# Two-layer graph attention block, one core: the score matmuls of the two layers are placed elsewhere among the projections, and layer 2's gather stands two matmuls later

## Chip, cores and metric

One Trainium2 chip, one of its NeuronCores. The metric is the device time of one execution in microseconds (us), the median over runs. The kernel holds 128 graphs of 128 nodes with 384 features each, all in float32, with the matmul operands split into two float32r parts.

## What is computed

For each graph with features h (128 x 384) and adjacency matrix A, two layers of

```
u     = h h^T / sqrt(384)
attn  = softmax(u) * A, each row divided by its sum
ctx   = (attn above the diagonal) (h Wl^T + bl) + diag(attn) (h Ws^T + bs)
        + (attn below the diagonal) (h Wr^T + br)
h'    = relu(layernorm(ctx) * g + beta)
```

and at the end `layernorm(x + h')`. The second layer reads the first one's output, so the two layers of one graph are dependent and different graphs are not.

## The kernel before, in words

Each engine has a program of its own, written out by hand and tied to the others by semaphores. All of them go through the same rounds i = 0 ... 132. A round works on layer 1 of graph i and on layer 2 of graph i-3 or so; the rounds 0 to 3 fill the pipeline, 127 on drain it, rounds 8 to 123 stand in a hardware loop unrolled four times. In this text k = 0 is layer 1 and k = 1 is layer 2, as in the code.

**TensorE in a round** (`iteration` of the tensor block) issues, before the change:

1. `project_sides(0, i)`: 18 projection matmuls of layer 1 (128x384 moving), nine for the upper and nine for the lower side. Each product of two float32 matrices is three matmuls on float32r parts (high x high, low x high, high x low), times three chunks of the 384 features.
2. `project_self(0, i)`: nine more for the self term. Among them `pair_slice` puts the score steps: matmuls 2, 3, 4 are each followed by one step of layer 1's scores of graph i+2, matmuls 5, 6, 7 each by one step of layer 2's scores of graph i-2. A score step (`score_step`, line 458) is one matmul with 256 moving columns over one of the three chunks.
3. `project_sides(1, i-3)`, steps 0 to 6; then `gather(1, i-4)`, six matmuls that apply layer 2's attention; then steps 7 to 17 of the same sides.
4. `project_self(1, i-3)`, nine matmuls; then `gather(0, i)`, six matmuls.

That makes 54 projections (line 464), 12 gather matmuls (line 584) and 6 score steps (line 458). Waits are put before the matmul that needs them: `gather(1, i-4)` waits for POOL's low part of the cut attention (`s_side_lo[1]`, line 1289) and for the low part of the projections; the score steps wait for the low part of the features that they read (`s_lo[0]` written by POOL at line 1319 for layer 1, `s_lo[1]` written by VectorE at line 745 for layer 2) and for `s_kept`, which says that ScalarE has copied the PSUM bank of the last scores away.

**VectorE in a round**: `normalise_layer1(i-1)` (lines 689 to 708), `low_rows(i-2)` (line 745), the bias of layer 1's sides (line 758, which waits for the last matmul of `project_sides(0, i)`), the scaled scores of both layers (line 769), a transposition, the masks (line 793) with their transpositions, the diagonals, and then the second half: the self bias, layer 2's rows (lines 689 to 716) after `gather(1)`, layer 2's bias (758), `output_rows` (724, 730), the self bias of layer 2 (762).

**ScalarE in a round**: the rectified rows (line 1074), their high part (1085), `normalise_rows` (1057), the two exponentials (1030), `high_sides(1, i-4)` (1044), `copy_cross(i)` (1016), `high_projections(0, i)` (1053), `high_sides(0, i)` (1044), `keep_high(i)` (1024, 1025; it raises `s_kept`), the load of transposed rows, `high_input` (1124; the high part of a new graph's features), small ones, `finish` (1057), `high_projections(1, i-3)` (1053).

**POOL in a round**: `low_projections(1, i-4)` (line 299), the layer norm's root and bias, the sum of crossed scores (1345), the cuts of both attention matrices (1283), `low_sides(1, i-4)` and `low_sides(0, i)` (1289), `low_projections(0, i)` (299), two more roots (1293), and at the end `low_input` (1319; the low part of a new graph's features).

**SyncE** issues the transfers in order; the features of graph i+4 (`xt_raw<-xT`) are asked for at the start of round i, once `s_lo[0]` of graph i+2 is there.

The high part of graph i+3's features is made by ScalarE in round i, its low part by POOL at the end of round i; four slots (`hT_layer1`) hold them.

Of the kernel before, what the change touches and what calls it, by code (L numbers as in the profile page):

```python
# [52 lines left out]
def graph_block(nc: bass.Bass, xT: bass.AP, x: bass.AP, adj: bass.AP, WT: bass.AP, bias: bass.AP,  # L53
                gain_cols: bass.AP, shift_cols: bass.AP, gain_row: bass.AP, shift_row: bass.AP, out: bass.AP):
    G, N, D = x.shape
    C = D // P
# [6 lines left out]
    with ExitStack() as ctx:  # L63
# [129 lines left out]
        def per_layer(name):  # L193
            return [sem(f"{name}1"), sem(f"{name}2")]
# [3 lines left out]
        s_lo = per_layer("s_lo")  # L198
        s_parts = per_layer("s_parts")
# [6 lines left out]
        s_kept = sem("s_kept")  # L206
# [37 lines left out]
        def live(i, b):  # L244

            return not isinstance(i, int) or 0 <= b < G

        def done(eng, s, b):

            if not isinstance(b, int) or b >= 0:  # L250
                eng.wait_ge(s, b + 1)
# [43 lines left out]
        def low_projections(op, eng, k, b):  # L295

            u = unit(k, b)
            done(eng, s_proj_hi[k], b)
            op.tensor_tensor(proj_split[u][:, LO], proj[u][:, UP:LOW + 1, :],  # L299
                             proj_split[u][:, HI].bitcast(F32), ALU.subtract).then_inc(s_proj_lo[k], 1)  # L300

        def filling(i):

            return isinstance(i, int) and i < 4
# [149 lines left out]
        def _(pe):  # L454
            def score_step(k, b, slot, n):

                h = hT_of(k, b)
                return nc.tensor.matmul(parts[k], h[:, slot, HI, n, :],  # L458
                                        h[:, slot, HI:LO + 1, n, :], start=(n == 0), stop=(n == C - 1))

            def project_step(k, b, slot, which, n):

                c, (mv, st) = n // 3, TERMS[n % 3]
                return nc.tensor.matmul(p_proj[:, which, 0:D], hT_of(k, b)[:, slot, st, c, :],  # L464
                                        w[:, k, which, mv, c, :], start=(n == 0), stop=(n == 8))
# [16 lines left out]
                    nc.tensor.matmul(parts[k][:, HI, :], cross[k][:], ident_r[:], start=False,  # L482
                                     stop=True, skip_group_check=True).then_inc(s_score[k], 1)

            def pair_slice(b0, slot0, b1, slot1, n):

                if n == 2:
                    if isinstance(b1, int) and b1 == 2:  # L490
                        done(pe, s_negmax[0], 5)
                        done(pe, s_negmax[1], 1)
                    else:
                        done(pe, s_kept, b1 - 3)
                    if b0 is not None:
                        done(pe, s_lo[0], b0)
                if b0 is not None and 2 <= n < 2 + C:
                    step = score_step(0, b0, slot0, n - 2)
                    if n == 1 + C:
                        step.then_inc(s_parts[0], 1)  # L500
                if n == 2 + C:
                    done(pe, s_lo[1], b1)
                if 2 + C <= n < 2 + 2 * C:
                    step = score_step(1, b1, slot1, n - 2 - C)
                    if n == 1 + 2 * C:
                        step.then_inc(s_parts[1], 1)

            def project_sides(k, b, slot, before, b_last, steps, scored=None, first=0, last_part=14):

                if 0 in steps:
                    done(pe, s_biased[before], b_last)
                for n in steps:
                    if isinstance(b, int) and b == 0 and n % 3 == 0:

                        pe.wait_ge(s_w_lo[k][UP + n // 9], n % 9 // 3 + 1)
                    last = project_step(k, b, slot, UP + n // 9, n % 9)
                    if scored is not None:  # L520
                        score_slice(*scored, n, first, last_part)
                if 17 in steps:
                    last.then_inc(s_proj[k], 1)

            def project_self(k, b, slot, before, b_last, scored=None, first=0, last_part=8, pair=None):
                done(pe, s_self_biased[before], b_last)
                for n in range(9):
                    if isinstance(b, int) and b == 0 and n % 3 == 0:
                        pe.wait_ge(s_w_lo[k][SELF], n // 3 + 1)
                    last = project_step(k, b, slot, SELF, n)  # L530
                    if pair is not None:
                        pair_slice(*pair, n)
                    if scored is not None and n < 8:
                        score_slice(*scored, n, first, last_part)
                last.then_inc(s_self[k], 1)
                if scored is not None:
                    score_slice(*scored, 8, first, last_part)
# [122 lines left out]
            def iteration(i, r):  # L660
                p, q = r % 2, 1 - r % 2
                if filling(i):
                    fill(i, p)
                elif closing(i):
                    close(i, p)
                else:
                    b0 = i + 2 if live(i, i + 2) else None
                    project_sides(0, i, r, 1, i - 4, range(18))
                    project_self(0, i, r, 1, i - 4, pair=(b0, (r + 2) % 4, i - 2, p))
                    project_sides(1, i - 3, q, 0, i, range(7))  # L670
                    gather(1, i - 4)
                    project_sides(1, i - 3, q, 0, i, range(7, 18))
                    project_self(1, i - 3, q, 0, i)
                    gather(0, i, True)

# [328 lines left out]
        def _(act):  # L1004
# [115 lines left out]
            def high_input(b, slot):  # L1120
                moved(act, s_xt, b, slot % 2)

                done(act, s_self[0], b - 4)
                nc.scalar.activation(hT[0][:, slot, HI], xt_raw[:, slot % 2], ACT.Copy).then_inc(s_hi[0], 1)  # L1124
# [123 lines left out]
            def iteration(i, r):  # L1248
                p, q = r % 2, 1 - r % 2
                if filling(i):  # L1250
                    fill(i, p, q)
                    return
                if closing(i):
                    close(i, p, q)
                    return
                relu_rows(i, i - 2, p)
                high_rows(i - 2, p)
                normalise_rows(i, i - 1)
                exponentials(1, i - 3, q)
                if live(i, i + 1):  # L1260
                    exponentials(0, i + 1, q)
                high_sides(1, i - 4)
                copy_cross(i)
                high_projections(0, i)
                high_sides(0, i)
                keep_high(i)
                load_rows(i - 1, q)
                if live(i, i + 3):
                    high_input(i + 3, (r + 3) % 4)
                if live(i, i + 1):  # L1270
                    squared_denominators(0, i + 1, q)
                squared_denominators(1, i - 3, q)
                if live(i, i - 5):
                    output_squares(i - 5, q)
                    finish(i, q)
                high_projections(1, i - 3)
# [4 lines left out]
        def _(pool):  # L1281
# [4 lines left out]
            def low_sides(k, b):  # L1286
                u = unit(k, b)
                done(pool, s_side_hi[k], b)
                nc.gpsimd.tensor_tensor(AT_split[u][:, LO], AT[u][:], AT_split[u][:, HI].bitcast(F32),  # L1289
                                        ALU.subtract).then_inc(s_side_lo[k], 1)  # L1290
# [26 lines left out]
            def low_input(b, slot):  # L1317
                done(pool, s_hi[0], b)
                nc.gpsimd.tensor_tensor(hT[0][:, slot, LO], xt_raw[:, slot % 2], hT[0][:, slot, HI].bitcast(F32),  # L1319
                                        ALU.subtract).then_inc(s_lo[0], 1)  # L1320
# [87 lines left out]
            def iteration(i, r):  # L1408
                p, q = r % 2, 1 - r % 2
                if filling(i):  # L1410
                    fill(i, p, q)
                    return
                if closing(i):
                    close(i, p, q)
                    return
                low_projections(nc.gpsimd, pool, 1, i - 4)
                deviation_layer1(i - 1)
                attn_arrived(i - 1, q)
                if not isinstance(i, int) or i > 4:
                    add_cross(0, 2)  # L1420
                cut_sides(1, i - 4)
                cut_sides(0, i)
                low_sides(1, i - 4)
                low_sides(0, i)
                low_projections(nc.gpsimd, pool, 0, i)
                deviation_layer2(i - 4)
                if live(i, i - 5):
                    deviation_output(i - 5, q)
                if live(i, i + 3):
                    low_input(i + 3, (r + 3) % 4)  # L1430

            run(pool, iteration)

# [31 lines left out]
```

## Time and profile before

| | |
|---|---|
| median of 3 runs | 1624.32 us (1623.67 to 1625.14) |
| the profiled execution's own time | 1624.36 us |
| its span, first to last instruction | 1622.6 us |
| granted TensorE clock | 0.998 |
| busy: TensorE, VectorE, ScalarE, POOL | 99%, 86%, 67%, 80% |
| projections, gathers, score steps | 6912, 1536, 768 matmuls |

How to read it: PE is TensorE's matmuls, PEld its weight loads, DVE VectorE, ACT ScalarE. In a timeline row the columns are start and duration in us, engine, line, operation, what is written and read, the shape, and how many instructions of one kind in a row were merged (x21); a bracket tells how long the engine was idle before and what ended that. A matmul's recorded duration (0.34 us for 384 columns) is longer than the distance to the next one's start, since they are pipelined; so the pace of n merged matmuls is (duration - 0.34) / (n - 1).

### The profile page before, as it was taken

How to read it: one execution, taken by the hardware profiler on the slowest of the kernel's cores; microseconds unless marked ns; L12 is line 12 of the kernel's file. 1: busy time of each engine (PE TensorE's matmuls, PEld its weight loads, DVE VectorE, ACT ScalarE, POOL GpSimd, SP SyncE). 2: the span in 40 equal slices, each digit the busy share in tenths (PEclk: the TensorE clock that was granted, in tenths of full speed). 3: DMA queues.
4: the chain of work that ended last, by engine and by line, in shares of the span. 5: the costliest groups of instructions: out<-in, count | busy, mean ns of one | idle time of the engine just before them, and what ended most of it. 6: DMA issues, size and time to landing. Idle time of an engine off the chain costs nothing.

```text
span 1622.6 us, 35792 instructions
## 1 busy us (share of the span) xinstructions
PE 1604.5 (99%) x9267; PEld 1579.7 (97%) x9267; DVE 1397.6 (86%) x4490; ACT 1079.5 (67%) x2958; POOL 1294.3 (80%) x1665
## 2 busy tenths in 40 slices
PE   9999999999999999999999999999999999999996
PEld 8999999999999999999999999999999999999995
DVE  7888888888888888888888888888888888888887
ACT  6666666666666666666666666666666666666665
POOL 6788888888878888888888888888888888888874
PEclk9999999999999999999999999999999999999999
DMA  5555555555555555555555555555555555555541
GB/s 184 124 138 130 132 128 139 127 132 128 139 126 133 129 137 126 134 134 131 131 130 133 131 134 128 134 132 134 128 137 130 132 128 139 127 133 129 133 107 49
DMA packets 589175, 211.28 MB, mean 130 GB/s; under 512 B 473952, under 2 KB 572256, under 8 KB 589152
## 3 DMA queue, kind: packets, MB, share of 16 engines
q1 hardware_dynamic: 490752, 198.91, 47.5%
q10 hardware_dynamic: 98400, 12.11, 4.8%
q8 instruction: 9, 0.15, 0.0%
q14 instruction: 14, 0.11, 0.0%
HBM read 128.98 MB, written 81.92 MB: 130 GB/s over the span
## 4 chain that ended last, share of the span: by engine, by line
PE 96%; POOL 1%; DVE 1%; ACT 1%; issue 1%; DMA 0%; ACTq 0%; DVEq 0%; SPq 0%; POOLq 0%
PE p_proj L464 73%; PE p_gather L584 17%; PE p_score L458 5%; POOL proj_split L299 0%; DMA w_raw<-WT 0%; POOL w L1340 0%; POOL rstd L1293 0%; ACT proj_split L1053 0%; DMA rows_mem<-rows_blocks 0%; POOL attnT_split L1289 0%; DVE proj L758 0%; ACT spread L1112 0%; DVE p_gather L716 0%; ACT p_score L1030 0%; DVE p_gather L724 0%
## 5 line engine op out<-in xcount | busy, mean ns | idle before, releaser
L464 PE MATMUL p_proj<-w,hT_layer 128*128 128x384 f32 x6912 | 1352.5, 339 | 0.0
L464 PEld LDWEIGHTS p_proj<-w,hT_layer 128*128 128x128 f32 x6912 | 1221.7, 188 | 0.2
L299 POOL TENSOR_TENSOR proj_split<-proj,proj_split 128x768 fp32r<-128x768 f32 x253 | 467.2, 1846 | 88.1 <-ACT proj_split L1053 88.1
L584 PE MATMUL p_gather<-proj_split,attnT_split 128*128 128x384 f32 x1536 | 324.0, 345 | 1.8 <-issue 1.5
L758 DVE TENSOR_TENSOR proj<-p_proj,bias_all 128x768 f32<-128x768 f32 x256 | 243.8, 952 | 79.1 <-PE p_proj L464 79.0
L1289 POOL TENSOR_TENSOR attnT_split<-attnT,attnT_split 128x256 fp32r<-128x256 f32 x256 | 189.8, 741 | 152.3 <-ACT attnT_split L1044 152.2
L584 PEld LDWEIGHTS p_gather<-proj_split,attnT_split 128*128 128x128 f32 x1536 | 264.7, 188 | 23.3 <-POOL attnT_split L1289 21.2
L1293 POOL TENSOR_TENSOR rstd<-veps,neg_half 128x1 f32<-128x1 f32 x384 | 209.5, 549 | 56.3 <-DVE veps L702 40.7
L1053 ACT ACTIVATE proj_split<-proj 128x768 fp32r<-128x768 f32 x256 | 213.0, 832 | 5.2 <-DVE proj L758 4.2
L458 PE MATMUL p_score<-hT_layer 128*128 128x256 f32 x768 | 215.2, 281 | 1.1 <-DVE hT_layer L745 0.8
L1057 ACT ACTIVATE normed<-gathered,nbias,rstd 128x384 f32<-128x384 f32 x128 | 90.7, 709 | 140.3 <-POOL nbias L1297 140.3
L1057 ACT ACTIVATE o<-y,nbias,rstd 128x384 f32<-128x384 f32 x128 | 90.8, 709 | 133.0 <-POOL nbias L1297 133.0
L1283 POOL TENSOR_TENSOR attnT<-whole,sides 128x256 f32<-128x256 f32 x249 | 178.8, 739 | 0.3 <-DMA whole<-swap_mem 0.3
L1124 ACT ACTIVATE hT_layer<-xt_raw 128x384 fp32r<-128x384 f32 x128 | 67.2, 525 | 144.7 <-issue 143.7
L1074 ACT ACTIVATE p_rows<-rowsT,shift,gain 128x128 f32<-128x128 f32 x369 | 149.4, 444 | 0.0
L1030 ACT ACTIVATE p_score<-scores,rows 128x128 f32<-128x128 f32 x256 | 92.8, 363 | 83.8 <-DVE rows L769 83.8
L458 PEld LDWEIGHTS p_score<-hT_layer 128*128 128x128 f32 x768 | 144.9, 189 | 1.9 <-DVE hT_layer L745 1.1
L762 DVE TENSOR_TENSOR proj<-p_proj,bias_all 128x384 f32<-128x384 f32 x256 | 141.5, 553 | 1.8 <-PE p_proj L464 1.7
L1319 POOL TENSOR_TENSOR hT_layer<-xt_raw,hT_layer 128x384 fp32r<-128x384 f32 x128 | 131.3, 1026 | 2.5 <-ACT hT_layer L1124 2.5
L793 DVE CUSTOM_DVE_ANT_0 attn<-p_score,adj_layer 128x128 f32<-128x128 f32 x256 | 70.9, 277 | 44.6 <-ACT p_score L1030 42.4
L1044 ACT ACTIVATE attnT_split<-attnT 128x256 fp32r<-128x256 f32 x256 | 103.3, 403 | 0.5 <-DVE attnT L822 0.5
L689 DVE SCALAR_TENSOR_TENSOR p_gather<-proj,rows,p_gather 128x384 f32<-128x384 f32 x128 | 79.6, 622 | 19.9 <-PE p_gather L584 12.5
(69 smaller groups left out, 1677.7 us busy)
## 6 DMA issues: line engine op xcount, KB each, us to landing
swap_mem<-blocks SPq DMA_DIRECT2D x124, 256.0 KB, 2.2
whole<-swap_mem SPq DMA_DIRECT2D x496, 64.0 KB, 2.5
xt_raw<-xT SPq DMA_DIRECT2D x128, 192.0 KB, 2.8
xn<-x SPq DMA_DIRECT2D x128, 192.0 KB, 2.7
out<-o SPq DMA_DIRECT2D x128, 192.0 KB, 2.0
rows_mem<-rows_blocks SPq DMA_DIRECT2D x123, 192.0 KB, 1.9
adj_layer<-adj SPq DMA_DIRECT2D x256, 64.0 KB, 2.1
rowsT<-rows_mem SPq DMA_DIRECT2D x246, 48.0 KB, 2.6
```

The costliest lines, as they stand in the source:

```text
L299: op.tensor_tensor(proj_split[u][:, LO], proj[u][:, UP:LOW + 1, :], proj_split[u][:, HI].bitcast(F32), ALU.subtract).then_inc(s_proj_lo[k], 1)
L458: return nc.tensor.matmul(parts[k], h[:, slot, HI, n, :], h[:, slot, HI:LO + 1, n, :], start=(n == 0), stop=(n == C - 1))
L464: return nc.tensor.matmul(p_proj[:, which, 0:D], hT_of(k, b)[:, slot, st, c, :], w[:, k, which, mv, c, :], start=(n == 0), stop=(n == 8))
L584: last = nc.tensor.matmul(home(k, b)[:, 0:D], AT_split[u][:, st, side, :], proj_split[u][:, mv, side, :], start=(side == UP and n == 0), s ...
L758: nc.vector.tensor_tensor(proj[u][:, UP:LOW + 1, :], p_proj[:, UP:LOW + 1, 0:D], bias_all[:, k, UP:LOW + 1, :], ALU.add).then_inc(s_biased ...
L762: nc.vector.tensor_tensor(proj[u][:, SELF, :], p_proj[:, SELF, 0:D], bias_all[:, k, SELF, :], ALU.add).then_inc(s_self_biased[k], 1)
L1053: nc.scalar.activation(proj_split[u][:, HI], proj[u][:, UP:LOW + 1, :], ACT.Copy).then_inc(s_proj_hi[k], 1)
L1057: nc.scalar.activation(rows_out, rows_in, ACT.Identity, bias=nbias[:, which:which + 1], scale=rstd[:, which:which + 1]).then_inc(s_rows, 1)
L1074: last = nc.scalar.activation(relu_T[:, c, :], rows_in[:, c, :], ACT.Relu, bias=shift1[:, c:c + 1], scale=gain1[:, c:c + 1])
L1283: nc.gpsimd.tensor_tensor(AT[k][:], whole[:, k].unsqueeze(1).broadcast_to([P, 2, N]), sides[:], ALU.mult).then_inc(s_side[k], 1)
L1289: nc.gpsimd.tensor_tensor(AT_split[u][:, LO], AT[u][:], AT_split[u][:, HI].bitcast(F32), ALU.subtract).then_inc(s_side_lo[k], 1)
L1293: return nc.gpsimd.tensor_tensor(rstd[:, which:which + 1], veps[:, which:which + 1], neg_half[:], ALU.pow)
```

## The change

The score steps are taken out of `pair_slice` and spread:

- Layer 1's scores of a graph take three steps in three places. The first (chunk 0) for graph i+3 is issued in round i, behind matmul 9 of `project_sides(1, i-3)`, which is the first after `gather(1, i-4)`. The other two (chunks 1 and 2), for graph i+2, follow matmuls 1 and 3 of `project_sides(0, i)`. In rounds 4 and 5 all three stand in `project_sides(0, i)`, behind matmuls 1, 3 and 5.
- Layer 2's three steps (graph i-2) follow matmuls 0, 1 and 2 of `project_self(0, i)`.
- `gather(1, i-4)` follows steps 0 to 8 of `project_sides(1, i-3)`, not 0 to 6.
- The features are prepared a graph earlier: `high_input` and `low_input` work in round i on graph i+4, not i+3. In round 4 both do graph 7 too, POOL's before `low_projections(0, 4)`.

```diff
-            def pair_slice(b0, slot0, b1, slot1, n):
-                if n == 2:
...
+            def score_early(b0, slot0, chunk):
+                if chunk == 0:
+                    done(pe, s_lo[0], b0)
+                    if isinstance(b0, int) and b0 == 6:
                         done(pe, s_negmax[0], 5)
                         done(pe, s_negmax[1], 1)
                     else:
+                        done(pe, s_kept, b0 - 7)
+                step = score_step(0, b0, slot0, chunk)
+                if chunk == C - 1:
+                    step.then_inc(s_parts[0], 1)
+
+            def score_late(b1, slot1, n):
+                if n == 0:
+                    done(pe, s_lo[1], b1)
+                    if not isinstance(b1, int) or b1 > 2:
                         done(pe, s_kept, b1 - 3)
+                if n < C:
+                    step = score_step(1, b1, slot1, n)
+                    if n == C - 1:
                         step.then_inc(s_parts[1], 1)
...
                     last = project_step(k, b, slot, UP + n // 9, n % 9)
+                    if early is not None and (n, early[2]) == (9, 0):
+                        score_early(early[0], early[1], 0)
+                    if early is not None and n in (1, 3, 5) and early[2] > 0 and n // 2 + early[2] <= C:
+                        score_early(early[0], early[1], n // 2 + early[2] - 1)
...
-                    b0 = i + 2 if live(i, i + 2) else None
-                    project_sides(0, i, r, 1, i - 4, range(18))
-                    project_self(0, i, r, 1, i - 4, pair=(b0, (r + 2) % 4, i - 2, p))
-                    project_sides(1, i - 3, q, 0, i, range(7))
+                    alone = isinstance(i, int) and i < 6
+                    rest = (i + 2, (r + 2) % 4, 1 if alone else 2) if live(i, i + 2) else None
+                    first = (i + 3, (r + 3) % 4, 0) if live(i, i + 3) and not (isinstance(i, int) and i < 5) else None
+                    project_sides(0, i, r, 1, i - 4, range(18), early=rest)
+                    project_self(0, i, r, 1, i - 4, late=(i - 2, p))
+                    project_sides(1, i - 3, q, 0, i, range(9))
                     gather(1, i - 4)
-                    project_sides(1, i - 3, q, 0, i, range(7, 18))
+                    project_sides(1, i - 3, q, 0, i, range(9, 18), early=first)
                     project_self(1, i - 3, q, 0, i)
                     gather(0, i, True)
...
                 load_rows(i - 1, q)
-                if live(i, i + 3):
-                    high_input(i + 3, (r + 3) % 4)
+                if isinstance(i, int) and i == 4:
+                    high_input(7, 3)
+                if live(i, i + 4):
+                    high_input(i + 4, r)
...
                 low_sides(0, i)
+                if isinstance(i, int) and i == 4:
+                    low_input(7, 3)
                 low_projections(nc.gpsimd, pool, 0, i)
...
-                if live(i, i + 3):
-                    low_input(i + 3, (r + 3) % 4)
+                if live(i, i + 4):
+                    low_input(i + 4, r)
```

## Rows read from the trace of the kernel before

**Rows 1.** The page: busy time by engine, and TensorE's clock in 40 slices.
```profile
PE 1604.5 (99%) x9267; PEld 1579.7 (97%) x9267; DVE 1397.6 (86%) x4490; ACT 1079.5 (67%) x2958; POOL 1294.3 (80%) x1665
...
PEclk9999999999999999999999999999999999999999
```

**Rows 2.** Who waited for whom: us in total, times, longest.
```profile
DVE proj L758 <- PE p_proj L464: 79.0, 128, 1.0
...
PEld p_gather L584 <- POOL attnT_split L1289: 21.2, 122, 0.5
```

**Rows 3.** Timeline of TensorE in one round, which begins at 802.67.
```profile
802.67 3.87 PE L464 MATMUL p_proj<-w,hT_layer 128*128 128x384 f32 x21
...
806.38 0.28 PE L458 MATMUL p_score<-hT_layer 128*128 128x256 f32 x1
...
807.96 1.55 PE L464 MATMUL p_proj<-w,hT_layer 128*128 128x384 f32 x8
...
809.36 1.33 PE L584 MATMUL p_gather<-proj_split,attnT_split 128*128 128x384 f32 x6
...
810.54 3.70 PE L464 MATMUL p_proj<-w,hT_layer 128*128 128x384 f32 x20
...
814.07 1.21 PE L584 MATMUL p_gather<-proj_split,attnT_split 128*128 128x384 f32 x6
...
815.12 1.22 PE L464 MATMUL p_proj<-w,hT_layer 128*128 128x384 f32 x6
```

**Rows 4.** The same round, what stands between its sides and layer 2's gather.
```profile
806.05 0.96 DVE L758 TENSOR_TENSOR proj<-p_proj,bias_all 128x768 f32<-128x768 f32 x1 [0.63 <-PE p_proj L464]
...
806.99 0.28 DVE L769 CUSTOM_DVE_ANT_0 scores<-p_gather,cross_sum 128x128 f32<-128x128 f32 x1
...
807.31 0.37 ACT L1030 ACTIVATE p_score<-scores,rows 128x128 f32<-128x128 f32 x1 [0.68 <-DVE rows L769]
...
808.10 0.40 ACT L1044 ACTIVATE attnT_split<-attnT 128x256 fp32r<-128x256 f32 x1
...
808.57 0.73 POOL L1289 TENSOR_TENSOR attnT_split<-attnT,attnT_split 128x256 fp32r<-128x256 f32 x1 [0.61 <-ACT attnT_split L1044]
...
809.36 1.01 PEld L584 LDWEIGHTS p_gather<-proj_split,attnT_split 128*128 128x128 f32 x6 [0.17 <-POOL attnT_split L1289]
```

**Rows 5.** The same round: layer 2's new features, and the end of the kept scores.
```profile
804.86 0.56 DVE L745 TENSOR_TENSOR hT_layer<-p_rows,hT_layer 128x384 fp32r<-128x384 f32 x1
...
809.90 0.22 ACT L1025 ACTIVATE p_gather<-p_score 128x128 f32<-128x128 f32 x1
```

**Rows 6.** Timeline of TensorE elsewhere: projections in a row, start-up and drain.
```profile
14.73 2.76 PE L464 MATMUL p_proj<-w,hT_layer 128*128 128x384 f32 x15
```
```profile
1574.17 5.11 PE L464 MATMUL p_proj<-w,hT_layer 128*128 128x384 f32 x28
...
1580.05 0.28 PE L458 MATMUL p_score<-hT_layer 128*128 128x256 f32 x1
1580.17 0.86 PE L464 MATMUL p_proj<-w,hT_layer 128*128 128x384 f32 x4
```
```profile
19.73 0.87 PE L464 MATMUL p_proj<-w,hT_layer 128*128 128x384 f32 x4
```

**Rows 7.** Round 4: ScalarE's and POOL's end of the round, and layer 1's gather.
```profile
51.17 1.85 POOL L299 TENSOR_TENSOR proj_split<-proj,proj_split 128x768 fp32r<-128x768 f32 x1
...
53.80 1.01 POOL L1319 TENSOR_TENSOR hT_layer<-xt_raw,hT_layer 128x384 fp32r<-128x384 f32 x1
```
```profile
52.79 0.53 ACT L1124 ACTIVATE hT_layer<-xt_raw 128x384 fp32r<-128x384 f32 x1 [2.06 <-issue]
```
```profile
54.69 1.21 PE L584 MATMUL p_gather<-proj_split,attnT_split 128*128 128x384 f32 x6
```

**Rows 8.** Round 6: the latest of layer 2's new features, and the round's start.
```profile
70.96 0.56 DVE L745 TENSOR_TENSOR hT_layer<-p_rows,hT_layer 128x384 fp32r<-128x384 f32 x1 [0.61 <-ACT hT_layer L1085]
```
```profile
68.17 3.87 PE L464 MATMUL p_proj<-w,hT_layer 128*128 128x384 f32 x21
```

More of the change, by code:

```diff
@@ L483, in score_slice @@
                                      stop=True, skip_group_check=True).then_inc(s_score[k], 1)
-            def pair_slice(b0, slot0, b1, slot1, n):
-                if n == 2:
-                    if isinstance(b1, int) and b1 == 2:
+            def score_early(b0, slot0, chunk):
+                if chunk == 0:
+                    done(pe, s_lo[0], b0)
+                    if isinstance(b0, int) and b0 == 6:
                         done(pe, s_negmax[0], 5)
@@ L493, in pair_slice, with project_sides @@
                     else:
-                        done(pe, s_kept, b1 - 3)
[L495 to L505, printed above, removed]
+                        done(pe, s_kept, b0 - 7)
[6 more added lines that the diff above has]
+                    if not isinstance(b1, int) or b1 > 2:
+                        done(pe, s_kept, b1 - 3)
+                if n < C:
+                    step = score_step(1, b1, slot1, n)
+                    if n == C - 1:
                         step.then_inc(s_parts[1], 1)
-            def project_sides(k, b, slot, before, b_last, steps, scored=None, first=0, last_part=14):
+            def project_sides(k, b, slot, before, b_last, steps, scored=None, first=0, last_part=14,
+                              early=None):
                 if 0 in steps:
@@ L523, in project_sides, with project_self @@
                     last.then_inc(s_proj[k], 1)
-            def project_self(k, b, slot, before, b_last, scored=None, first=0, last_part=8, pair=None):
+            def project_self(k, b, slot, before, b_last, scored=None, first=0, last_part=8, late=None):
                 done(pe, s_self_biased[before], b_last)
@@ L530, in project_self @@
                     last = project_step(k, b, slot, SELF, n)
-                    if pair is not None:
-                        pair_slice(*pair, n)
+                    if late is not None:
+                        score_late(*late, n)
                     if scored is not None and n < 8:
```

## Prediction, made before the changed kernel was run

> **What bounds the kernel now.** The page comes first: TensorE is busy 99% of the span, at its full clock in every slice (the higher of its two levels, 2.4 GHz), the next engine 86% [rows 1]. So only two things can give time back: a place where TensorE waits, and the pace at which its matmuls follow each other. The list of waits shows the one wait that comes back in every round: the weight load of layer 2's gather stands until POOL has written the low part of the cut attention, 21.2 us in 122 times, 0.17 us each [rows 2]. TensorE's timeline shows what that costs: layer 2's gather takes 1.33 us where layer 1's, which waits for nothing, takes 1.21 [rows 3]. So 0.12 us of a round are lost (the remaining 0.05 of the late load hide behind the running matmul), 122 x 0.12 = 14.6 us in all. A round lasts 815.12 - 802.67 = 12.45 us [rows 3].
>
> Then the pace. Projections in a row follow each other at (3.87 - 0.34) / 20 = 0.1765 us at the round's start and at (3.70 - 0.34) / 19 = 0.1768 behind layer 2's gather, but at (1.55 - 0.34) / 7 = 0.1729 behind the last score step [rows 3]. I call these the slow and the fast pace; they differ by 0.0037 us. The fast one is no matter of layer or weights: in the start-up 15 projections of layer 1 run at (2.76 - 0.34) / 14 = 0.1729, and in the drain 28 in a row run at (5.11 - 0.34) / 27 = 0.1767 and, once three score steps have come between, at (0.86 - 0.34) / 3 = 0.173 [rows 6]. One row speaks against a simple rule: behind the scores that follow a gather in the start-up, four run at (0.87 - 0.34) / 3 = 0.177 [rows 6]. A score step costs this: from 806.38 to 807.96 are six of them and five projections, 1.58 us, less 5 x 0.1765, by six: 0.116 us [rows 3].
>
> **The change part by part.** No matmul is added or removed: 54 P, 12 gathers and 6 scores stay in a round. P is 0.1765 and S is 0.116.
>
> *The gather, two steps later, and the scores ahead of it.* What does the gather wait for? Rows 4, read upwards: POOL's operation waited for ScalarE, which waited for VectorE's scores, which follow its bias addition with no pause, and that one had been idle for 0.63 us until TensorE's last matmul of layer 1's sides. This wait is there 128 times [rows 2]. The last of those 18 matmuls starts at 802.67 + 17 x 0.1765 = 805.67 and ends 0.34 later, 806.01; the gather's load starts at 809.36. So the gather is ready 3.35 us after the end of the sides, whatever TensorE does between. Before, TensorE would have wanted that load at 33 P + 6 S = 6.52 us of the round and had it at 6.69: 0.17 late, as the row says. After, two scores stand inside the sides, so all that chain starts 2 S = 0.23 later and the load is ready at 6.92. TensorE wants it at 35 P + 5 S = 6.76: 0.16 late. Two projections put in front (0.35) are paid back by one score that leaves that stretch (0.12) and two that delay the chain (0.23). The stall stays: 0 us, with 0.01 x 122 = 1.2 us as the most that the rounding of these rows allows either way.
>
> *Everything behind shifts alike.* VectorE's work behind layer 2's gather, and what ScalarE and POOL do after it, moves 0.23 later in the round, and so does the end of layer 1's sides that it must be ready for: the 0.63 us of idle time [rows 4] stays. SyncE's queue asks for no other transfers, and at the same places; its wait on `s_lo[0]` only gets easier. Cost 0, covered by that 0.63.
>
> *New waits.* (a) Layer 2's first score follows projection 0 of the self term and waits for VectorE's low rows. They end at 804.86 + 0.56 - 802.67 = 2.75 in the round, 3.04 after the shift and a signal of 0.06; TensorE wants the weights at 18 P + 2 S = 3.41. There are 0.37 us to spare, where there was about 1 us. Cost 0; behind it in TensorE's queue stands all of the rest. (b) The early score behind the gather waits for ScalarE's kept scores, which end at 809.90 + 0.22 = 810.12, 0.76 after the gather's load starts [rows 4, 5]; TensorE wants the weights when the projection ahead of the score starts, 1.18 after it (810.54 in this round [rows 3]). Both hang on the same chain, so 1.18 - 0.76 - 0.06 = 0.36 us stay. Cost 0. (c) POOL's low input for it was made a round before. Cost 0. ScalarE's `high_input` now needs the self term of the same round, which ended at about 807.96 plus one and a half projections; it runs at 811.3. Cost 0.
>
> *The pace.* This is the term that I take to be worth something. In layer 1's sides two scores now stand behind matmuls 1 and 3, in the position of the drain's case (slow before, fast after [rows 6]), so matmuls 4 to 17 should run at the fast pace: 14 x 0.0037 = 0.05 us a round, in 121 rounds (5 to 125) 6.3 us; I take 6.1, one round less sure at each end. A faster pace between the sides and the gather gives nothing, for the gather waits for the chain. Behind the gather stands one score; if the 15 projections behind it ran fast too, that would be 15 x 0.0037 x 121 = 6.7 us more. That one is nearest the start-up row which stayed slow, so I count 0 and keep 6.7 for the range. Nothing excludes a loss: a score costs up to 0.120 in place of 0.116, 121 x 2 x 0.004 = 1 us.
>
> What the rows show here is a projection at 0.1729 or at 0.1767 by what ran before it. The Trainium skill (TensorE: Matmul & The Clock Gate, section Wait — 56ns, not 53.3ns?) says otherwise: back-to-back matmuls are N / 2.4 GHz plus a fixed 2.5 ns or so, 162.5 ns for 384 columns. By that rule no order of scores changes the pace, and the term would be 0. The trace agrees with neither the size nor the fixedness.
>
> *Round 4, once.* POOL makes graph 7's low input before `low_projections(0, 4)`. It can begin when ScalarE's copy ends, 52.79 + 0.53 = 53.32, takes 1.01 and ends at 54.33; the projections' low part takes 1.85, to 56.18, where it began at 51.17 before. Layer 1's gather, which wanted its weights at 54.69 - 0.17 = 54.52, gets them 1.7 us late [rows 7]. Cost 1.7 us; bounds 0 (if the rounds behind catch up) and 2.5 (if the roots queued behind on POOL, and VectorE's output rows that wait for them, are late in round 5 too).
>
> **Sum.** Against the profiled execution's own 1624.36 us (span 1622.6 and 1.8 around it; the median of the runs is 1624.32, so nothing is to be moved): -6.1 + 1.7 = -4.4, **1620.0 us**.
>
> **The rivals.**
> - *Both paces turn fast.* -6.1 - 6.7 + 1.7: 1613.3 us. For it: a fast stretch in the start-up lasts 15 matmuls. Against it: the row at 19.73 [rows 6]. Chance 0.22.
> - *The pace does not hang on the scores.* Then nothing is left but round 4 and the score's own price: 1624.4 + 1.7, 1626.1 us (to 1627). For it: slow behind scores in the start-up; the skill's rule would say the same. Against it: 122 rounds with 0.1729 behind the last score. Chance 0.27.
> - *The change does what its words suggest.* The gather's two steps hide its wait: 14.6 us off, 1624.4 - 14.6 + 1.7 = 1611.5 us. It needs a chain that does not start at the sides' end; 128 waits of VectorE for TensorE speak against it. Chance 0.05.
> - *Slower: the late scores wait for the low rows.* Place: the first score in `project_self(0, i)`. It decides once VectorE ends line 745 more than 0.37 us later in the round than now, which happened in round 6: 70.96 + 0.56 - 68.17 = 3.35 [rows 8]. If every round were like it: ready at 3.35 + 0.23 + 0.06 = 3.64, 0.23 late, 0.16 of it seen; 0.12 is given back at the gather, which has that much less to wait, and since the gather's chain hangs on the sides only 0.04 to 0.09 a round are left, 5 to 11 us: 1632 us beside the pace's rival. Chance 0.08.
>
> **How the numbers follow.** The forecast has 0.38. The range takes in it, the two pace rivals with round 4's bounds, and most of the hidden wait: 1612.5 to 1627.5, leaving out the slower case and the far ends. About 0.2% (3.2 us) is what a measurement of this kernel can tell from no change, so faster means below 1621.1. The forecast lies only 1.1 us under that, so a quarter of its chance counts as same: faster 0.28 + 0.22 + 0.05 = 0.55; same 0.10 + 0.23 = 0.33; slower 0.04 + 0.08 = 0.12.
>
> **What would show it.** In the changed profile: TensorE's row behind the second score in layer 1's sides, 15 projections (14 and the self term's first) at 0.173 and not 0.177; the weight load of layer 2's gather still idle before it for 0.16 to 0.19 us, 121 times, on POOL; VectorE's 0.6 us idle before line 758 as before; a round of 12.40 us; and once, at about 55 us, a wait of 1.7 us for POOL's line 299. Wrong I would be if that load's wait were gone, if scores waited on VectorE's line 745 or ScalarE's 1025, or if the pace in the sides stayed at 0.1765.

## The result, and the profile after

The changed kernel takes 1614.55 us (median of 6 runs, 1613.59 to 1615.10) against 1624.43 us of the kernel before on the same chips (1623.67 to 1625.42): ratio 0.9938, 95% interval 0.9925 to 0.9950. That is 9.9 us less, where the forecast was 4.4 less (1620.0 us) and the range 1612.5 to 1627.5.

The page of the changed kernel, against [rows 1]:

```profile
span 1613.0 us, 35972 instructions
...
PE 1594.6 (99%) x9267; PEld 1571.5 (97%) x9267; DVE 1396.4 (87%) x4490; ACT 1079.3 (67%) x2958; POOL 1294.1 (80%) x1665
```

The matmuls are the same 9267, and 9.9 us of TensorE's busy time are gone. "Busy" is the union of pipelined matmuls here, so this is a change of pace, which no list of waits shows. The waits, against [rows 2]:

```profile
DVE proj L767 <- PE p_proj L464: 71.6, 127, 1.1
...
PEld p_gather L591 <- POOL attnT_split L1300: 14.3, 92, 0.2
```

VectorE still waits for the end of layer 1's sides, 71.6 / 127 = 0.56 us a round (79.0 / 128 = 0.62 before). The weight load of layer 2's gather still waits for POOL. The longest single wait is 0.2 us; it is listed 92 times, but the gather is late in every round: its second matmul starts 0.269 us or more behind the first in all 119 rounds that are compared below, and 0.176 us (median) behind it where the stall is gone (experiment 3). One round on TensorE's timeline, against [rows 3], and then its weight load:

```profile
802.89 2.81 PE L464 MATMUL p_proj<-w,hT_layer 128*128 128x384 f32 x15
805.54 1.32 PE L591 MATMUL p_gather<-proj_split,attnT_split 128*128 128x384 f32 x6
...
806.99 3.17 PE L464 MATMUL p_proj<-w,hT_layer 128*128 128x384 f32 x17
810.00 1.21 PE L591 MATMUL p_gather<-proj_split,attnT_split 128*128 128x384 f32 x6
811.05 0.52 PE L464 MATMUL p_proj<-w,hT_layer 128*128 128x384 f32 x2
...
811.99 2.76 PE L464 MATMUL p_proj<-w,hT_layer 128*128 128x384 f32 x15
814.59 0.28 PE L458 MATMUL p_score<-hT_layer 128*128 128x256 f32 x1
```
```profile
805.54 0.99 PEld L591 LDWEIGHTS p_gather<-proj_split,attnT_split 128*128 128x128 f32 x6 [0.16 <-POOL attnT_split L1300]
```

Layer 1's sides with the first self matmul, 19 projections and two scores, take 814.59 - 811.05 = 3.54 us; at the slow pace they would take 19 x 0.1765 + 2 x 0.116 = 3.59. The fifteen behind the second score run at (2.76 - 0.34) / 14 = 0.1729. Behind the late scores, which have one projection between them, fifteen run at (2.81 - 0.34) / 14 = 0.1764: that stretch was fast before and is slow now. The gather takes 1.32 us, 0.11 more than layer 1's: its stall is there (before: 0.12), and the load is 0.16 us late, as forecast. Behind it 17 projections run at (3.17 - 0.34) / 16 = 0.177 in this round. In five of the six rounds from 607 to 674 us, though, that row is shorter; one of each kind:

```profile
609.30 3.12 PE L464 MATMUL p_proj<-w,hT_layer 128*128 128x384 f32 x17
...
621.65 3.17 PE L464 MATMUL p_proj<-w,hT_layer 128*128 128x384 f32 x17
```

3.12 is (3.12 - 0.34) / 16 = 0.1738 a projection: fast. The last twelve projections of that row run at 0.1733 in 84 of the 119 rounds and at 0.1767 in the other 35. Over all unrolled and looped rounds (119 after, 122 before) the mean start-to-start times add up as follows, in us:

| stretch of a round | before | after | plain slow pace would give after |
|---|---|---|---|
| layer 1's sides, with the scores in them | 3.181 | 3.371 | 3.181 + 0.232 = 3.413 |
| from there to the gather's second matmul | 3.800 | 3.802 | |
| the rest of the gather | 0.885 | 0.879 | |
| from the gather to layer 1's gather | 3.535 | 3.264 | 3.535 - 2 x 0.1765 + 0.116 = 3.298 |
| layer 1's gather | 1.046 | 1.044 | |
| sum | 12.446 | 12.360 | |

The second line is the chain: two projections more and three scores fewer stand in that stretch, and it lasts the same to 0.002 us. The experiments show why: the gather is bound by what began at the sides' end. The change's gain lies in the first and fourth lines, 0.042 and 0.034 us of pace, plus 0.006 in the gather; that is 0.082 of the 0.086 us, and the rest is no more than P and S are rounded by. 0.086 x 120 = 10.3 us, less one wait of 0.9 us in round 4, gives 9.4 of the 9.9 us. The wait:

```profile
50.68 1.21 PE L591 MATMUL p_gather<-proj_split,attnT_split 128*128 128x384 f32 x6
...
55.81 1.28 PE L591 MATMUL p_gather<-proj_split,attnT_split 128*128 128x384 f32 x6 [0.74 <-issue]
```

### The profile page after: what moved, and what is told of

Same layout as the page of the kernel before. It is cut to its first block, busy times and chain, and to the rows that moved or that the text cites. A ratio compares the mean times of both kernels' runs of the same rounds, so it can differ in the third digit from the quotient of the medians.

```text
span 1613.0 us, 35972 instructions
## 1 busy us (share of the span) xinstructions
PE 1594.6 (99%) x9267; PEld 1571.5 (97%) x9267; DVE 1396.4 (87%) x4490; ACT 1079.3 (67%) x2958; POOL 1294.1 (80%) x1665
## 4 chain that ended last, share of the span: by engine, by line
PE 97%; DVE 1%; POOL 1%; ACT 1%; issue 0%; DMA 0%; SPq 0%; DVEq 0%; POOLq 0%; ACTq 0%
PE p_proj L464 74%; PE p_gather L591 17%; PE p_score L458 5%; DMA w_raw<-WT 0%; POOL proj_split L299 0%; POOL w L1351 0%; DVE proj L767 0%; DVE p_gather L725 0%; DVE p_gather L733 0%; DVE stats L702 0%; DVE p_gather L698 0%; ACT proj_split L1062 0%; PE p_score L482 0%; DVE y L739 0%; POOL rstd L1304 0%
## 5 line engine op out<-in xcount | busy, mean ns | idle before, releaser
L464 PEld LDWEIGHTS p_proj<-w,hT_layer 128*128 128x128 f32 x6912 | 1193.7, 188 | 0.5 <-POOL w L1351 0.3
L767 DVE TENSOR_TENSOR proj<-p_proj,bias_all 128x768 f32<-128x768 f32 x256 | 243.9, 953 | 71.6 <-PE p_proj L464 71.6
```

Source lines behind the costliest of these rows:

```text
L767: nc.vector.tensor_tensor(proj[u][:, UP:LOW + 1, :], p_proj[:, UP:LOW + 1, 0:D], bias_all[:, k, UP:LOW + 1, :], ALU.add).then_inc(s_biased ...
```

## Experiments

Two theories stood against each other. **Chain and pace**: layer 2's gather is ready a fixed time after the end of layer 1's sides; the gain comes from which projections run at the fast pace. **Gather**: the gain comes from the gather's later place, as the change's words suggest.

**1. The gather back in its old place.** One edit to the changed kernel:

```diff
-                    project_sides(1, i - 3, q, 0, i, range(9))
+                    project_sides(1, i - 3, q, 0, i, range(7))
                     gather(1, i - 4)
-                    project_sides(1, i - 3, q, 0, i, range(9, 18), early=first)
+                    project_sides(1, i - 3, q, 0, i, range(7, 18), early=first)
```

> The changed kernel with layer 2's gather back behind 7 sides matmuls, all else as changed. Theory (the gather is ready a fixed 3.35 us after the end of layer 1's sides, and two scores stand in those sides): TensorE reaches the gather two projections (0.35 us) earlier and waits that much longer, 0.10 + 0.35 = 0.45 us a round, 121 x 0.35 = 42 us more than the changed kernel's 1614.6: 1657 us. Rival (the gain is the pace alone and the gather's place is of no account): 1615 us. Second rival (the gather's readiness moves with what TensorE does just before it, not with the sides' end): 1615 to 1625 us.

Measured: 1655.72 us (1655.48 to 1656.31), ratio to before 1.0189 (1.0174 to 1.0205). Its weight loads:

```profile
800.89 1.00 PEld L591 LDWEIGHTS p_gather<-proj_split,attnT_split 128*128 128x128 f32 x6 [0.50 <-POOL attnT_split L1300]
```

The load is 0.50 us late, where it was 0.16, and 41.2 us were lost where 42 were forecast. The gather does not get ready any sooner when TensorE comes sooner. By the mean round the stretch from the sides' end to the gather's second matmul is 3.805 us, against 3.802 in the changed kernel. So the two steps are no gain of their own: they pay for the two scores put ahead of the sides' end and the one that left the stretch.

**2. The gather's move alone**, in the kernel before:

```diff
-                    project_sides(1, i - 3, q, 0, i, range(7))
+                    project_sides(1, i - 3, q, 0, i, range(9))
                     gather(1, i - 4)
-                    project_sides(1, i - 3, q, 0, i, range(7, 18))
+                    project_sides(1, i - 3, q, 0, i, range(9, 18))
```

> The kernel before with only layer 2's gather moved behind 9 sides matmuls; the scores stay in the self term. Theory: nothing stands in layer 1's sides, so the gather is ready at the same time and TensorE reaches it 0.35 us later, after it is ready: the 0.12 us of stall go, the pace stays slow: 1624.4 - 122 x 0.12 = 1610 us, a round of 12.33 us. Rival (the gather's readiness slides with TensorE): the load's wait stays, 1624 us. Rival (VectorE becomes the bound, since layer 2's second half starts 0.23 us later in the round): 1615 to 1625 us with waits of TensorE for line 758 or 745.

Measured: 1607.59 us (1606.68 to 1608.15) against 1624.73 before, ratio 0.9895 (0.9880 to 0.9910). Its weight-load waits and a round:

```profile
PEld p_gather L584 <- POOL attnT_split L1289: 0.6, 3, 0.3
```

```profile
811.71 1.90 PE L464 MATMUL p_proj<-w,hT_layer 128*128 128x384 f32 x10
813.44 1.20 PE L584 MATMUL p_gather<-proj_split,attnT_split 128*128 128x384 f32 x6
```

122 waits have become 3 and the gather takes 1.20 us. Without scores ahead of the sides' end the move does hide the stall, and this one edit is worth 17.1 us, more than the whole change. That is 2.5 us more than the 14.6 forecast. The mean round is 12.303 us, 0.142 less than before (0.142 x 122 = 17.3 us). Of this the gather gives 0.120, as forecast; the last projection ahead of it, which the stall had drawn out from 0.174 to 0.190, gives 0.016; and the two projections moved ahead of the gather give 0.007, since they joined the fast stretch behind the last score, (1.90 - 0.34) / 9 = 0.1733 for ten of them. So the stall had cost 0.136 us a round, a little more than the 1.33 - 1.21 by which it was priced. Had VectorE been near its limit it would have shown here; no wait for it came.

**3. The changed kernel with the gather one step later still** (`range(10)` and `range(10, 18)`, and the early score behind matmul 10):

> The changed kernel with layer 2's gather one step later still, behind 10 sides matmuls, and the early score right behind the next one. Theory: the load of that gather is 0.16 us late in the changed kernel; one projection of 0.177 covers it, so 0.10 us a round go: 1614.6 - 121 x 0.10 = 1602.5 us, and no wait for POOL's line 1300 is left in the list. Rival (readiness slides with TensorE): 1614.6 us. Rival (something else is late next, the kept scores or layer 2's low rows): 1605 to 1612 us, with its name in the list of waits.

Measured: 1601.64 us (1600.85 to 1601.84), ratio 0.9858 (0.9842 to 0.9873). A round and the wait:

```profile
808.36 2.99 PE L464 MATMUL p_proj<-w,hT_layer 128*128 128x384 f32 x16
811.19 1.21 PE L591 MATMUL p_gather<-proj_split,attnT_split 128*128 128x384 f32 x6
```

```profile
PEld p_gather L591 <- POOL attnT_split L1300: 0.2, 1, 0.2
```

The forecast was 1602.5: one projection covers the 0.16 us. Nothing else is late next.

**4. Round 4's order on POOL.**

```diff
-                if isinstance(i, int) and i == 4:
-                    low_input(7, 3)
                 low_projections(nc.gpsimd, pool, 0, i)
+                if isinstance(i, int) and i == 4:
+                    low_input(7, 3)
```

> The changed kernel with POOL's low input of graph 7 in round 4 put behind low_projections(0, 4). Theory: the one wait of 0.9 us ahead of layer 1's gather in round 4 goes and nothing is put in its place: 1614.6 - 0.9 = 1613.7 us. Rival: TensorE waits for something else as long in round 5 (the three early scores of graph 7, or VectorE): 1614.6 us.

Measured: 1612.79 us (1612.00 to 1613.50), ratio 0.9924 (0.9911 to 0.9938), 1.8 us under the changed kernel; the two intervals overlap, so the size is not settled. In the timeline the distance between the two gathers falls from 55.81 - 50.68 = 5.13 us to

```profile
50.91 1.21 PE L591 MATMUL p_gather<-proj_split,attnT_split 128*128 128x384 f32 x6
...
55.14 1.21 PE L591 MATMUL p_gather<-proj_split,attnT_split 128*128 128x384 f32 x6
```

4.23 us. These 0.90 us are shown. The two profiled executions are only 1613.50 and 1614.73 us, 1.2 apart, and 119 rounds that are 0.003 us shorter in the mean (12.356 for 12.359) make 0.4 of it; the rest of the 1.8 between the medians was not located.

**5. The pace by itself.** The two early scores of the changed kernel later in the same sides, nothing else:

```diff
-                    if early is not None and n in (1, 3, 5) and early[2] > 0 and n // 2 + early[2] <= C:
-                        score_early(early[0], early[1], n // 2 + early[2] - 1)
+                    if early is not None and n in (13, 15, 17) and early[2] > 0 and (n - 12) // 2 + early[2] <= C:
+                        score_early(early[0], early[1], (n - 12) // 2 + early[2] - 1)
```

> The changed kernel with the two early scores of layer 1's sides behind matmuls 13 and 15 instead of 1 and 3: the same matmuls, the same count of scores ahead of the sides' end, the gather in its place. Theory (a score puts the projections behind it on the fast pace of 0.1733 us; ahead of it they run at 0.1767): twelve projections more run slowly, 12 x 0.0034 x 121 = 4.9 us: 1614.6 + 4.9 = 1619.5 us. Rival (the pace comes from something else in the changed kernel, and the scores' place within the sides is of no account): 1614.6 us.

Measured: 1617.56 us (1616.88 to 1618.86), ratio 0.9963 (0.9949 to 0.9976) with 1624.08 before; 3.0 us over the changed kernel by the medians, 4.1 by the ratios to the kernel before, (0.9963 - 0.9938) x 1624. In the profile:

```profile
799.80 2.28 PE L464 MATMUL p_proj<-w,hT_layer 128*128 128x384 f32 x12
...
807.84 3.12 PE L464 MATMUL p_proj<-w,hT_layer 128*128 128x384 f32 x17
```

Twelve projections ahead of the scores run at (2.28 - 0.34) / 11 = 0.1764, slow, where the changed kernel has 0.1729. The same matmuls in the same number ahead of the same chain: the scores' place sets the pace of what follows. By the mean round layer 1's sides take 3.411 for 3.371 us, the 0.040 that was forecast. But the whole round is 12.380 us, only 0.021 over the changed kernel's, which is 2.5 us over 120 rounds and not 4.9: the stretch behind the gather takes 3.251 for 3.264, because here it runs fast in all 119 rounds and not in 84, and the gather gives the other 0.006. Why the stretch behind the gather changed too was not found.

**6. Late scores with two projections between them**, on top of 3 (gather behind 10):

```diff
-                if n < C:
-                    step = score_step(1, b1, slot1, n)
-                    if n == C - 1:
+                if n in (0, 2, 4):
+                    step = score_step(1, b1, slot1, n // 2)
+                    if n == 4:
```

> The kernel with the gather behind 10 sides matmuls (1601.6 us), and layer 2's late scores behind self matmuls 0, 2 and 4 instead of 0, 1 and 2. Theory (two projections between scores keep the fast pace, one does not): the fifteen projections up to the gather run at 0.1733 instead of 0.1767, 0.05 us a round; the gather is reached that much earlier, still within what hides: 1601.6 - 6 = 1595.5 us. Rival (the load of the gather is late again, so the pace is given back): 1599 to 1602 us, with POOL's line 1300 back in the list of waits. Rival (the spacing of the scores does not set the pace): 1601.6 us.

Measured: 1597.67 us (1596.97 to 1598.76), ratio 0.9838 (0.9824 to 0.9851). A round:

```profile
806.74 0.28 PE L458 MATMUL p_score<-hT_layer 128*128 128x256 f32 x1
806.86 2.60 PE L464 MATMUL p_proj<-w,hT_layer 128*128 128x384 f32 x14
809.30 1.23 PE L591 MATMUL p_gather<-proj_split,attnT_split 128*128 128x384 f32 x6
```

The stretch between the last late score and the gather turns from (2.99 - 0.34) / 15 = 0.1767 (experiment 3) to (2.60 - 0.34) / 13 = 0.1738. By the medians 4.0 us came of the 6 forecast, by the ratios to the kernel before 3.2, (0.9858 - 0.9838) x 1624. The mean round says the latter: 12.216 for 12.243 us, 0.027 x 119 = 3.2. The stretch up to the gather gains 0.047, nearly the 0.05 forecast; the gather, now reached earlier, takes 1.23 and not 1.21 us, so part is given back there.

**7. Gather behind 11, late scores behind 0, 2, 4, round 4 as in 4.**

> All together: the gather behind 11 sides matmuls, the late scores behind self matmuls 0, 2 and 4, and graph 7's low input behind low_projections(0, 4). Theory: no wait for POOL in any round, fast pace nearly everywhere, the one wait of round 4 shorter: 1595.5 - 1.8 = 1593.7 us. Rival (VectorE's second half, now 0.35 us later than in the changed kernel, makes something wait: its line 754 or 767, or POOL's line 299 ahead of layer 1's gather): 1596 us or more, with that name in the list.

Measured: 1598.72 us (1598.10 to 1600.12), ratio 0.9843 (0.9830 to 0.9857), where the theory had 1593.7: the rival. The list of waits has it only in part, since each wait is shorter than what it counts, but the timeline shows the place:

```profile
815.81 0.19 PEld L458 LDWEIGHTS p_score<-hT_layer 128*128 128x128 f32 x1
...
818.01 0.56 DVE L754 TENSOR_TENSOR hT_layer<-p_rows,hT_layer 128x384 fp32r<-128x384 f32 x1
...
818.62 0.19 PEld L458 LDWEIGHTS p_score<-hT_layer 128*128 128x128 f32 x1
818.71 0.30 PE L458 MATMUL p_score<-hT_layer 128*128 128x256 f32 x1
```

VectorE's low rows end at 818.57, and the load of the first late score starts 0.05 us after. They end 3.38 us into the round (median over the rounds), 2.76 in the kernel before. The first late score and what precedes it take 0.028 us more a round than in experiment 6 (means over 119 rounds: 0.182 + 0.138 for 0.173 + 0.119). This is the slower rival of the prediction, at its place, once the gather stands 0.35 us later still.

**8 and 9. The two ways out of it.** 8 is experiment 6 with the edit of 4. 9 is experiment 7 with the late scores one step later:

```diff
-                if n == 0:
+                if n == 1:
                     done(pe, s_lo[1], b1)
...
-                if n in (0, 2, 4):
-                    step = score_step(1, b1, slot1, n // 2)
-                    if n == 4:
+                if n in (1, 3, 5):
+                    step = score_step(1, b1, slot1, n // 2)
+                    if n == 5:
```

> The kernel with the gather behind 10 and the late scores behind 0, 2, 4 (1597.7 us), plus graph 7's low input behind low_projections(0, 4). Theory: the wait of 0.95 us ahead of layer 1's gather in round 4 goes: 1596.7 us. Rival (that wait was not what the other kernel with this edit gained by): 1597.7 us.

> The kernel with the gather behind 11 sides matmuls, the late scores behind self matmuls 1, 3 and 5 instead of 0, 2 and 4, and graph 7's low input behind low_projections(0, 4). Theory: in the kernel with 0, 2, 4 the first late score waits 0.03 us a round for VectorE's line 754, which ends later in the round since the gather stands later; one self matmul more (0.173) covers it: 1598.7 - 0.03 x 121 = 1595 us, and 1594 if the uneven pace behind it goes as well. Rival (the 0.03 us are not a wait for line 754): 1598.7 us.

Measured: 8 takes 1595.70 us (1595.49 to 1596.33), 9 takes 1595.68 (1595.02 to 1596.36), both with ratio 0.9820 (0.9806 to 0.9833). In 9 the score's waits for line 754 are

```profile
PEld p_score L458 <- DVE hT_layer L754: 1.6, 2, 1.1
```

two, both single ones, and 3.0 us are back by the medians, 3.7 by the ratios; the theory had 1595. For 8 the forecast was 1596.7, from the 0.95 us of round 4 alone; 2.0 came by the medians. The distance between round 4's gathers falls from 5.00 to 4.05 us, the 0.95; the mean round, 12.210 for 12.216 us, makes another 0.7. Either is 29 us under the kernel before and 19 under the changed one, with the same 9267 matmuls.

## Why the prediction was right, and where it was off

**Which stall stays.** Right, and by its own arithmetic: the load was to be 0.16 late and is 0.16. Its price was a little low, 0.12 us a round where experiment 2 shows 0.136, but as the stall stays this enters the forecast nowhere. The 3.35 us from the sides' end held too; the stretch up to the gather kept its length to 0.002 us, and experiments 1 to 3 moved the gather against it by -2, +2 and +1 projections with 41, 17 and 13 us as the answer.

**The pace in the sides.** Right: forecast 14 x 0.0037 = 0.05 us a round, measured 0.042, 5.1 us for 6.1.

**The pace behind the gather.** This is the term that was mis-sized. The prediction put "0" for it and kept 6.7 us for the range, because a start-up row with four projections behind scores stayed slow. Measured: 0.034 us a round, about 4.1 us, since the fifteen turn fast in 84 of 119 rounds. Four matmuls were too short a row to judge by: in experiment 5's trace the starts behind that score are 0.177, 0.176, 0.175 and 0.176 us apart before they settle at 0.173 to 0.174, and the start-up row's four are 0.178, 0.176, 0.175 and 0.176. It had not stayed slow; it ended too soon to show. So "both paces turn fast" (1613.3 us, chance 0.22) came nearer than the forecast. That the time lies within the range is owed to these 6.7 us having been kept in it.

**Round 4.** Placed right, too large: 1.7 us forecast, 0.9 measured. The working had POOL's extra operation begin when ScalarE's copy of graph 7 ends, at 53.32 as before. It began at 52.91:

```profile
52.91 1.02 POOL L1330 TENSOR_TENSOR hT_layer<-xt_raw,hT_layer 128x384 fp32r<-128x384 f32 x1 [2.29 <-ACT hT_layer L1133]
53.88 1.83 POOL L299 TENSOR_TENSOR proj_split<-proj,proj_split 128x768 fp32r<-128x768 f32 x1
```

The projections' low part ends at 55.71, not 56.18, since ScalarE's `copy_cross(4)` had waited 0.73 us for scores in the kernel before and waits for none now that they come early: a wait that the working did not look at. TensorE, which has three scores in that round's sides, also came 0.2 us later itself.

**New waits.** None in the changed kernel, as costed. The low rows end 3.02 us into the round (median), for 2.98 forecast; experiment 7 shows how near the limit is. One figure of that part is off, without weight in the sum: by its own terms the spare time before the change was 23 P + 3 S less 2.81, 1.6 us and not about 1.

**The fixed price per matmul.** The Trainium skill's rule (TensorE: Matmul & The Clock Gate, Wait — 56ns, not 53.3ns?) would have given no gain from order. That rule is a fixed cost of about 2.5 ns on each matmul besides its columns. Experiment 5 contradicts its fixedness for these float32r matmuls: order alone moved 3 us, and the twelve projections from 0.1729 to 0.1764 us each.

## What to carry to other kernels

When TensorE is 99% busy, divide merged rows of equal matmuls by their count: a difference of 2% between stretches is worth as much as a wait. Before moving work past a wait, find the event that the wait's chain starts from, and count what the move puts ahead of that event as well as ahead of the wait; here two projections bought nothing because two score matmuls went ahead of the chain's start and a third left the stretch, and one projection more was worth 13 us. Then move until the next thing is late, and stop one step short of it.

## What the hardware showed that was not expected

Projections of 384 columns follow each other at 0.1733 or at 0.1767 us, by what ran before them. At the start of a round in the kernel before, behind a gather, they alternate between 0.174 and 0.179; in the changed kernel two score matmuls with two projections between them bring them to 0.1733 there, and that lasts as long as the row does (14 in experiment 6; in the start-up fifteen run so too). Scores in alternation with single projections left the row behind them slow after three scores (fifteen projections, the changed kernel) and fast after six (eight, the kernel before; ten in experiment 2). A single score behind the gather was enough in all 119 rounds of experiments 3 and 5, after four projections of 0.175 to 0.178.

In the changed kernel that same score brought the fast pace in 84 rounds and not in 35, and a few nanoseconds just before go with it: where the gather's second matmul starts 269 to 270 or 275 to 276 ns behind its first, the row behind the score is slow (35 rounds), and at 271 to 274 or from 277 on it is fast (84 rounds), without exception. The hardware loop issues every fourth round by the same instructions on the same buffers, and both paces occur at each of its four places (8, 9, 13 and 4 slow rounds of 29). So the operands' places in memory do not set the pace by themselves; something does that differs from one pass of the loop to the next, and it shows in those few nanoseconds. What it is was not found. A phase between weight loads and matmuls would fit, and so would other engines' accesses at that moment; no experiment set either on purpose.
